# GpSimd gathers six of eight input chunks and scatters seven of eight output chunks through a table of row numbers

## The reference, cut to what matters

```
x = x + 0.5 * ffn(layernorm(x))      # front
x = x + attention(layernorm(x))      # middle: causal, 16 heads of 16, its output normalized again
x = x + 0.5 * ffn(layernorm(x))      # back, same weights as the front

ffn(x): logits = x @ w_router.T + b_router           # 8 experts
        mask   = 1 for the two largest of the 8 logits, else 0
        y      = sum over e of mask[e] * (x @ w_experts[e].T + b_experts[e])
```

## Time and profile before

| | us |
|---|---|
| run 1 | 983.14 |
| run 2 | 980.9 |
| median | 982.02 |
| span of the profiled execution | 980.6 |

### The profile page before, as it was taken

How to read it: one execution, slowest core, us unless ns; L and a number is a source line. 1 busy time by engine, 2 the same in 40 slices (tenths; PEclk the granted TensorE clock), 3 DMA queues, 4 the chain that set the end, 5 groups by cost and what they waited for, 6 DMA issues and landing times.

```text
span 980.6 us, 17661 instructions
## 1 busy us (share of the span) xinstructions
PE 948.2 (97%) x5602; PEld 564.8 (58%) x5602; DVE 824.3 (84%) x2445; ACT 511.1 (52%) x1053; POOL 259.5 (26%) x286
## 2 busy tenths in 40 slices
PE   6999999999999999999999999999988999999998
PEld 5778887776776333333333333333344777787776
DVE  5876777787697999999999999999767888888765
ACT  5325424414316677777777777777775334333210
POOL 1112214202203222222222212222343554434310
PEclk9999999999999999999999999999999999999999
DMA  6301121101114322333322222223320122110001
GB/s 224 96 1 65 65 66 65 65 1 65 54 44 132 99 78 78 79 78 79 76 76 66 71 64 66 65 70 79 98 58 13 44 66 65 64 64 22 1 22 43
DMA packets 55121, 64.37 MB, mean 66 GB/s; under 512 B 13830, under 2 KB 37366, under 8 KB 55030
## 3 DMA queue, kind: packets, MB, share of 16 engines
q1 hardware_dynamic: 54444, 62.52, 22.2%
q10 hardware_dynamic: 592, 0.80, 0.2%
HBM read 41.30 MB, written 21.23 MB: 64 GB/s over the span
## 4 chain that ended last, share of the span: by engine, by line
PE 87%; DVE 6%; ACT 3%; issue 2%; DMA 1%; SPq 1%; POOL 1%; DVEq 0%; ACTq 0%; POOLq 0%
PE bank L368 40%; PE bank L1654 14%; PE bank L1475 13%; PE bank L1636 13%; PE bank L873 3%; PE bank L360 2%; DVE bank L1502 1%; ACT b_probs L1610 1%; DMA v_all<-L_ffn_w_experts 1%; PE bank L815 1%; DVE a_acc L1109 1%; DVE b_neg L1506 0%; PE bank L802 0%; DVE a_st L320 0%; DVE a_rest L1120 0%
## 5 line engine op out<-in xcount | busy, mean ns | idle before, releaser
L1610 ACT ACTIVATE b_probs<-bank 128x512 f32<-128x512 f32 (+1 forms) x608 | 302.7, 585 | 111.0 <-PE bank L1636 110.4
L1502 DVE CUSTOM_DVE_ANT_0 bank<-bank,b_below 128x384 f32<-128x384 f32 (+3 forms) x512 | 235.5, 516 | 7.9 <-PE bank L1475 6.4
L1475 PE MATMUL bank<-b_ks,b_qs 96*128 96x512 bf16 (+3 forms) x768 | 220.8, 328 | 9.0 <-issue 5.1
L1636 PE MATMUL bank<-b_qs,b_ks 99*128 99x512 bf16 (+3 forms) x768 | 213.0, 328 | 4.8 <-ACT b_probs L1610 4.7
L368 PE MATMUL bank<-we,a_xt 128*128 128x512 f32 x768 | 192.6, 402 | 1.6 <-DVE a_acc L1109 1.2
L368 PE MATMUL bank<-we,c_xt 128*128 128x512 f32 x768 | 186.1, 398 | 0.4 <-DVE c_acc L1109 0.4
L1581 POOL TENSOR_SCALAR_AFFINE_SELECT b_probs<-b_probs 128x512 f32<-128x512 f32 x128 | 84.6, 661 | 310.7 <-ACT b_probs L1610 310.5
L1506 DVE TENSOR_REDUCE b_neg<-bank 128x1 f32<-128x512 f32 x256 | 161.2, 680 | 2.6 <-PE bank L1475 1.2
L368 PEld LDWEIGHTS bank<-we,c_xt 128*128 128x128 f32 x768 | 142.3, 188 | 32.2 <-DVE c_acc L1109 0.6
L368 PEld LDWEIGHTS bank<-we,a_xt 128*128 128x128 f32 x768 | 140.9, 189 | 29.8 <-DVE a_acc L1109 1.9
L1654 PE MATMUL bank<-b_probs,b_vs 128*32 128x512 f32 (+3 forms) x1536 | 155.1, 498 | 1.6 <-POOL b_probs L1581 1.6
(11 more groups left out here) (142 smaller groups left out, 905.9 us busy)
## 6 DMA issues: line engine op xcount, KB each, us to landing
b_qs<-q_parts SPq DMA_DIRECT2D x96, 128.0 KB, 3.0
b_ks<-k_parts SPq DMA_DIRECT2D x96, 128.0 KB, 3.0
q_parts<-a_part SPq DMA_DIRECT2D x16, 384.0 KB, 2.6
k_parts<-a_part SPq DMA_DIRECT2D x16, 384.0 KB, 2.7
att_num<-b_oev SPq DMA_DIRECT2D x64, 64.0 KB, 2.2
c_num<-att_num SPq DMA_DIRECT2D x8, 512.0 KB
c_rec<-att_rec SPq DMA_DIRECT2D x16, 256.0 KB
out<-xs SPq DMA_DIRECT2D x7, 512.0 KB, 3.2
```

Of the source, the lines that this page charges most:

```text
L1475: last = nc.tensor.matmul(ms[bank][:, a * width:(a + 1) * width], qs[g.u][0:ROWS, c, i * P:(i + 1) * P], ks[g.u][0:ROWS, c, lo:lo + width] ...
L1502: last = dve.tensor_tensor_reduce(part, part, below[:, CH - width:CH], -1.0, 3.0e38, ALU.add, ALU.min, dst[:, a, :])
L1610: act.activation(probs[b % 4][:, heads[0]:heads[0] + hp, 0:width], es[exp_bank(g, unit)][:, 0:hp * width].rearrange("p (h w) -> p h w", w= ...
L1636: last = nc.tensor.matmul(es[exp_bank(g, unit)][:, a * width:(a + 1) * width], ks[g.u][:, c, j * P:(j + 1) * P], qs[g.u][:, c, first_q:fir ...
```

## The change

A table `row_of` of row numbers (`row_of[p, n] = 128*n + p`) is made by POOL with one `iota`. POOL then fetches tiles 8 to 31 of `xs` (chunks 2 to 7) with 24 indirect transfers, each of 128 rows of 1 KB, all on the semaphore `x_in[2]`, for which DVE now waits until all 24 are in. They stand on POOL behind the constants and ahead of `clear_masks`. SP's transfer of 3 MB is gone. In the back POOL stores chunk `c` at the end of its slot with four indirect transfers, for chunks 0 to 6; SP's stores of these are gone, and SP waits at its end for both kinds. The last chunk is stored as before. The loop of the back's slots runs over slots 1 and 2 alone; slots 3 and 4 are written out.

```diff
+        s.row_of = sb("row_of", [P, NT], mybir.dt.int32)
+    s.x_rows = x.rearrange("b t d -> (b t) d")
+    s.out_rows = out.rearrange("b t d -> (b t) d")
...
-    pairs = 1 if first else 2
+    pairs = 1
...
-            load_x(2, 2, NCH)
...
-                else:
-                    sp.wait_ge(q.x_ready, at(TPC * c + TPC))
-                    sp.dma_start(s.out[:, tiles(c), :], s.xs[:, tiles(c), :]).then_inc(q.written, 16)
...
-            sp.wait_ge(q.written, at(16 * (NCH - 1 + TPC)))
+            sp.wait_ge(q.written, at(16 * TPC))
+            sp.wait_ge(q.rows_written, 16 * (NT - TPC))
...
             pool.memset(s.eps[:], EPS).then_inc(q.consts, 1)
+            pool.iota(s.row_of[:], pattern=[[P, NT]], base=0, channel_multiplier=1).then_inc(q.rows_ready, 1)
...
+            pool.wait_ge(q.rows_ready, 1)
+            for n in range(2 * TPC, NT):
+                pool.indirect_dma_start(s.xs[:, n, :], None, s.x_rows,
+                                        bass.IndirectOffsetOnAxis(ap=s.row_of[:, n:n + 1], axis=0)).then_inc(q.x_in[2], 16)
...
+        def store_rows(c):
+            pool.wait_ge(q.x_ready, at(TPC * c + TPC))
+            for t in range(TPC):
+                pool.indirect_dma_start(s.out_rows, bass.IndirectOffsetOnAxis(ap=s.row_of[:, TPC * c + t:TPC * c + t + 1], axis=0),
+                                        s.xs[:, TPC * c + t, :], None).then_inc(q.rows_written, 16)
...
                 add_tiles(c, (2,) if isinstance(c, int) and c == last_slot else (2, 3))
+                if exists(c + 1):
+                    store_rows(c)
...
-                dve.wait_ge(q.x_in[m], 16)
+                dve.wait_ge(q.x_in[m], 16 if m < 2 else 16 * (NT - 2 * TPC))
```

More of the change, by code:

```diff
@@ L199, in ffn @@
         q.later_in = once("later_in")
+        q.rows_ready = once("rows_ready")
         q.consts, q.bias_zero, q.bias_step, q.bias_placed = once("consts"), once("bias_zero"), once("bias_step"), once("bias_placed")
@@ L225, in ffn @@
         q.written, q.closing = sem("written"), sem("closing")
+        q.rows_written = ctx.enter_context(nc.semaphore("rows_written"))
     if first:
```

## The result

| | us |
|---|---|
| changed kernel, 2 runs | 994.36 and 998.44, median 996.4 |
| span of its profiled execution | 992.6 |
| kernel before, in the same comparison | median 982.02 |
| ratio, with its 95% interval | 1.0139 [1.0075, 1.0203] |

Timed again with four runs of the changed kernel and 23 of the kernel before it gave 1.0140 [1.0125, 1.0155] (experiment 1), 13.8 us. The forecast was 994.7 us, within the 2% called no change, and slower.

A forecast was written before the change was run, and what follows sets the result against it. PE, at work for 97% of the span, was taken as the bound. A mask delay of 11.0 us plus 1.7 us of clock gave 12.7 us, span 993.3 us, time 994.7 us (1.3% slower); range 981 to 1016 us.

The forecast's parts named there:

- the 2% called no change: Whole time: a change within 2% (19.6 us) either way counts as no change; chance 0.62.
- The place: At the start, gathers ahead of the mask memsets make DVE's first mask 11.0 us later, and PE waits as long.
- G: Time POOL is held by one indirect transfer of 128 rows, taken as 1.2 us, between 0.44 and 2.41 us.
- My lower end: Lower bound of POOL's hold per indirect transfer: 0.44 us, from SP's issue of the 3 MB transfer.
- The 1 us to the first byte: Alternative hold of POOL per gather at the start: the sum would be 4.8 us smaller, 989.9 us.
- The rival of rows fetched one by one: POOL at start and slot ends: 4.8 us a transfer, 1125 us in all; 10.9 us by the skill's figure; chance 0.07.
- The clock: Behind PE's idle wait at the start, a lower granted clock costs 1.7 us; lower end 0 if DVE limits that stretch.
- The wait for x: DVE's read of chunk 2 moves to 54.6 us; all gathers are in at 43.9 us, so this wait never decides.
- The weights' landing: First 14 us: gathers sharing DMA engines delay the weights a few us, covered by the 11 us wait for the masks.
- The scatters: End of each back slot: four scatters, 4.8 us of POOL, hidden in a hole of 5.19 us; cost 0.
- the slack: Back slots: 5.19 + 2.95 + 1.41 + 0.82 = 10.4 us of room, so scatters are free up to 2.6 us each.
- SP's freed queue and the loop: SP without the 3 MB load and the stores, and two back slots written out: each worth 0.

The follow-up runs named there:

- experiment 1: The whole change, unaltered, timed again with four runs against the kernel before: ratio 1.0140 [1.0125, 1.0155]; span 995.3 us.
- Experiment 2: The changed kernel with POOL zeroing the two mask tiles ahead of the 24 gathers: ratio to the kernel before 1.0003 [0.9993, 1.0013].
- experiment 11: The changed kernel with SP's 3 MB load back and 20 POOL memsets in the gathers' place: ratio to the kernel before 1.0133 [1.0119, 1.0148].
- experiment 8: The changed kernel with POOL's 24 fetches as plain transfers without the table: ratio to the kernel before 1.0093 [1.0071, 1.0114].
- experiment 10: The tripled kernel: the changed kernel with each scatter done three times, two into spare tensors; 1032.75 us, ratio to the kernel before 1.0506 [1.0484, 1.0528].
- experiment 3: Only the gathers of the change, SP storing the output chunks as before: ratio to the kernel before 1.0151 [1.0137, 1.0166].
- experiment 7: The changed kernel with 42 extra matmuls keeping PE busy while it would wait for the first mask: ratio to the kernel before 1.0149 [1.0132, 1.0166].
- experiment 4: Only the scatters of the change, SP loading chunks 2 to 7 in one transfer as before: ratio to the kernel before 1.0002 [0.9991, 1.0014].
- experiment 9: The doubled kernel: the changed kernel with each scatter done twice, the second into a spare tensor; 1004.88 us, ratio to the kernel before 1.0221 [1.0202, 1.0240].

## Why the prediction was right, point by point

**The place: right.** The gathers stand ahead of the mask memsets, DVE's first mask waits, and PE behind it. Experiment 2 shows that the order of two memsets against the gathers decides it, experiment 11 that twenty memsets which hold POOL as long do the same.

**G: 1.2 against 1.25 us.** The term was 11.0 us and measured 11.9 to 12.1. The choice between 0.44 and 2.41 us was by the nearest POOL row, and it fell close by some luck. My lower end was not out of reach: a plain fetch on POOL takes 0.55 us (experiment 8). The 1 us to the first byte, which the Trainium skill gives on the page "DMA: Bandwidth & Descriptors", section "Latency and other measured facts", is neither of the two holds measured here, 0.55 and 1.25 us. The rival of rows fetched one by one, 10.9 us a transfer, an estimate from the Trainium skill, page "GPSIMD Engine Reference", section "Performance pitfalls for Q7 kernels", did not show; 1.25 us is a ninth of it.

**The clock: mis-sized.** The fall of the clock came as forecast; its price was 0.35 us in the profiled execution and up to 1.26 us in another, not 1.7. The term assumed a stretch bound by PE, and it took 0.57 over the whole window from 704 to 708 us, though PE stood idle until 704.56 in it. In the changed kernel DVE was at work for 3.84 of the 4 us from 36 to 40 us, so the slower PE was probably hidden in part, which the prediction had named as its lower end. In experiment 10, where PE restarts behind a wait in the middle of a slot, 24 matmuls lost 1.6 to 2.8 us, so the size depends on the place. This error and that in G cancel: 11.0 + 1.7 = 12.7 forecast, 11.9 + 0.35 = 12.2 in the rows up to PE's second mask.

**From the rows to the time: 12.0 or 13.8 us.** The first profile's span grew by 12.0 us, the times by 13.8. The stretch between PE's seventh mask turn in the front (216 us before) and its first in the back (754 us) was 537.9 us before, 536.8 us in the first profile of the changed kernel, 538.7 in the second. The first was a lucky execution there by 1.1 us. Beyond the late mask and the clock, the whole times of experiments 1, 3, 7 and 11 hold another 0.6 to 2.4 us (by ratios that are known to about 1.5 us). No single place shows it: that same stretch, whose program no experiment touched, took 536.8 to 540.9 us in the fourteen profiles, which is more than what is sought. The prediction has no term for it, and it stays open.

**The wait for x: right.** It never decided. **The weights' landing: right, but thin.** PE's second quarter was 0.5 us later and hidden (1.8 us later in experiment 2, where nothing hid it). Experiment 8 shows how much the pace of the gathers, 128 KB in 1.25 us, had to do with that: at 128 KB in 0.55 us the weights decide.

**The scatters: right at 0, the slack wrong.** They cost nothing (experiment 4). POOL after the change, in the seam of the back (to the earlier trace rows):

```profile
797.18 0.74 POOL L507 TENSOR_TENSOR xs<-c_acc,c_acc 128x256 f32<-128x256 f32 x1 [7.41 <-DVE c_acc L1124]
798.20 1.06 POOL L513 DMA_INDIRECT out<-xs,row_of  x1 [0.28 <-POOL xs L507]
...
802.13 0.96 POOL L513 DMA_INDIRECT out<-xs,row_of  x1 [0.31 <-issue]
803.25 2.40 POOL L539 TENSOR_TENSOR c_yg<-c_yn,gamma 128x1024 f32<-128x1024 f32 x1 [0.15 <-ACT c_yn L347]
```

The hole of 5.19 us has become 0.15 us that still ends on ACT: the four scatters just fit into it. PE's mask turns in these slots stay 29.15 to 29.21 us apart. The prediction took the room, hole and all, to be 10.4 us; by the doubled kernel it is 8.4 to 8.9 us. Gaps alone were counted, and not that POOL and DVE, moved against each other, lengthen each other's instructions.

**SP's freed queue and the loop: right at 0**, by experiment 4, whose back has both and whose ratio is 1.0002 [0.9991, 1.0014]. The 0.44 us of issue that SP saves at the start are only in the kernels with the gathers.

## What to carry to other kernels

When transfers are issued from an engine that also computes, price the issue by the distance of two starts, count them up to the first small instruction that stands behind them in the program, and ask who waits for that one; moving two memsets was worth the whole loss here, to within what was measured. A slower issue can also be a protection: the faster plain fetches of experiment 8 delayed the weights that PE wanted. And a slack made of gaps on several engines is an upper bound, since shifting one engine against another changes what runs at the same time.

## What the runs showed of the hardware that was not expected

- An indirect transfer of 128 rows of 1 KB held POOL for 0.95 to 0.97 us (the first of a series up to 1.17) and 0.30 us more before the next, the same for gathers and scatters; a plain transfer of the same tile held it for 13.19/24 = 0.55 us. Beside DVE's 128x1024 product of two inputs in SBUF one scatter of the tripled kernel took 1.82 us.
- The 0.95 us were the same while the DMA engines were full (share 1.07 to 1.10 from 4 to 16 us in the changed kernel) and when they had less to do (0.32 from 28 to 32 us), so POOL was not waiting for them.
- The same program's granted clock behind the same idle stretch came back at different times: to the second mask turn 0.35 us were lost in one profile of the changed kernel and 1.26 us in the other, and 0.53, 0.76 and 0.99 us in experiments 9, 3 and 10, which have the same start.
